# Gating's second half moved to the end of the step, with its weights one step later, and the maxima transferred from another queue

## The reference

```
xn  = layernorm(x)
a   = softmax(rot(q) rot(k)^T / sqrt(8) + decay, causal) v      # 16 heads of 8
n1  = layernorm(xn) * w + b
rw  = gating(n1)                    # (tokens, 8 experts)
q, k, v = sum_e rw[e] * (n1 @ proj[e])
hs  = xn + sum_e rw[e] * (softmax(q k^T, causal) v) @ o_proj[e]
out = x + a @ Wo + hs + moe(layernorm(hs))

gating: l = normalize(n1) @ normalize(sim) - sigmoid(g)
        keep l > 0, or, where none is, the two largest l
        softmax over what is kept
```

## Time and profile before

| | |
|---|---|
| three runs | 1439.68 us median, 1435.52 to 1447.45 |
| profiled execution | 1432.54 us, its span 1430.7 us |
| PE busy | 1284.3 us, 90% of the span |
| PEld busy | 1016.5 us, 71% |
| DVE busy | 1021.5 us, 71% |
| ACT busy | 762.4 us, 53% |
| GpSimd busy | 221.6 us, 15% |

### The profile page before, as it was taken

One profiled execution on the slowest core, in us unless ns is written; L12 is line 12 of the kernel. 1 busy time (PEld: TensorE's weight loads), 2 busy tenths in 40 slices (PEclk: granted clock), 3 DMA queues, 4 the chain that ended last, 5 costly groups with the idle time before them and its releaser, 6 DMA issues.

```text
span 1430.7 us, 33751 instructions
## 1 busy us (share of the span) xinstructions
PE 1284.3 (90%) x10686; PEld 1016.5 (71%) x10780; DVE 1021.5 (71%) x3882; ACT 762.4 (53%) x1664; POOL 221.6 (15%) x326
## 2 busy tenths in 40 slices
PE   0369999999999999999999999999999979999999
PEld 0247777777778777777777777777777767777776
DVE  8557777777777777777777777777776656677754
ACT  1125655665555555555555555555555574455532
POOL 4011112111122211111111111112111200000000
PEclk9679999999999999999999999999999999999999
DMA  4423233223333333333222233223223204554344
GB/s 117 94 54 85 76 77 76 75 76 80 79 85 79 78 76 79 83 90 90 77 75 76 75 83 80 76 75 76 75 76 77 58 9 172 204 202 153 149 153 159
DMA packets 89904, 133.33 MB, mean 93 GB/s; under 512 B 9675, under 2 KB 78395, under 8 KB 78523
## 3 DMA queue, kind: packets, MB, share of 16 engines
q1 hardware_dynamic: 89298, 132.10, 32.6%
q10 hardware_dynamic: 488, 0.01, 0.0%
HBM read 108.76 MB, written 21.50 MB: 91 GB/s over the span
## 4 chain that ended last, share of the span: by engine, by line
PE 63%; DVE 15%; DMA 11%; issue 6%; ACT 4%; DVEq 1%; SPq 0%; ACTq 0%
DMA qst<-mT 10%; PE ps L1663 8%; PE ps L1649 8%; PE ps L1401 7%; PE ps L1402 6%; PE ps L1411 6%; PE ps L1275 4%; PE ps L1379 4%; DVE mx L1025 3%; PE ps L1337 3%; PE ps L1360 3%; PE ps L1333 2%; PE ps L1330 2%; PE ps L1436 1%; PE ps L1383 1%
## 5 line engine op out<-in xcount | busy, mean ns | idle before, releaser
L629 ACT ACTIVATE pr<-ps 128x512 f32<-128x512 f32 x384 | 227.7, 593 | 205.4 <-PE ps L1360 166.7
L1025 DVE TENSOR_REDUCE mx<-ps 128x2 f32<-128x512 f32 (+1 forms) x384 | 263.9, 688 | 46.6 <-PE ps L1330 26.2
L634 ACT ACTIVATE ps<-trn 128x512 f32<-128x512 bf16 x382 | 229.8, 601 | 12.1
L530 POOL TENSOR_TENSOR n1s<-rep,n1T 128x256 f32<-128x256 f32 x256 | 177.0, 730 | 277.4 <-DVE mpart L1037 252.9
L1663 PEld LDWEIGHTS ps<-w2s,ats 128*128 128x128 f32 x1024 | 131.7, 192 | 50.4 <-issue 46.5
L1401 PE MATMUL ps<-n1s,wq 128*128 128x256 f32 x512 | 160.6, 396 | 0.0
L1402 PE MATMUL ps<-n1s,wk 128*128 128x256 f32 x512 | 152.8, 380 | 0.0
L1411 PE MATMUL ps<-wv,n1s 128*128 128x128 f32 x1024 | 150.6, 280 | 0.0
L803 ACT ACTIVATE n1s<-ps 128x512 f32<-128x512 f32 x128 | 76.5, 597 | 123.3 <-PE ps L1649 122.1
L1411 PEld LDWEIGHTS ps<-wv,n1s 128*128 128x128 f32 x1024 | 131.9, 192 | 9.0 <-issue 6.3
L1663 PE MATMUL ps<-w2s,ats 128*128 128x128 f32 x1024 | 135.7, 276 | 1.1 <-DVE ats L1207 1.1
(11 more groups left out here) (225 smaller groups left out, 2281.6 us busy)
## 6 DMA issues: line engine op xcount, KB each, us to landing
rep<-scr_rw SPq DMA_DIRECT2D x32, 1024.0 KB, 5.0
qst<-scr_rw SPq DMA_DIRECT2D x16, 1024.0 KB, 6.5
kst<-scr_rw SPq DMA_DIRECT2D x16, 1024.0 KB, 8.3
scr_parts<-parts SPq DMA_DIRECT2D x64, 192.0 KB, 2.3
qst<-scr_parts SPq DMA_DIRECT2D x192, 64.0 KB
kst<-scr_parts SPq DMA_DIRECT2D x32, 192.0 KB
xt<-in_x SPq DMA_DIRECT2D x32, 128.0 KB, 2.3
kst<-scr_parts SPq DMA_DIRECT2D x32, 128.0 KB
```

What stands on the lines that cost most here:

```text
L530: pool.tensor_tensor(n1s[:, e], rep[:, par, e], n1T[:, par], ALU.mult).then_inc(n1s_done, 1)
L629: act.activation(pr[:, G % 2, i], ps[:, S2[k % 2]], ACT.Exp).then_inc(exp_done, 1)
L634: act.activation(ps[:, S2[k % 2]], seeds[:, 1 if (k + 2) % 3 == 2 else 0], ACT.Copy).then_inc(seed_done, 1)
L1025: dve.tensor_reduce(mx[:, min(i, 1), h:h + n], ps[:, S1[k % 2]].rearrange("p (h t) -> p h t", h=n), AX_X, ALU.max, negate=True).then_inc(s ...
```

## The change

Gating is cut in two. `gating_head` runs to the tanh's input in its old place, and only maxima 4 to 6 are put beside it. `gating_tail` runs at the end of the step, behind `add_x`, with `add_hs` put in behind link 24. `soft_max` now follows the layer norm, ahead of maxima 7 to 10, and `soft_norm` follows `max_parts`. The weights go through PE, ACT and SP one step later: `weights_T`, `evac_weights` and `store_weights` of sequence n + 1 stand early in step n, using the bank `PVB`, and `pv` of the step waits for the copy (`rwT_done`). `max_T` moves ahead of `soft_av`, `evac_max` ahead of `evac_v`, and the transfer of `mT` is issued by ACT itself instead of SP.

```diff
-GATE_MAX_AT = (3, 7, 10, 14, 18, 21, 24)
+GATE_MAX_AT = (3, 7, 10)
+HS_AT = 24
@@ SP, step
                 if n_x:
+                    store_weights(n + 1, 1 - u)
                     spread_weights(n + 1, 1 - u)
...
                     stacks(n + 2, u, True)
-                    store_weights(n + 2, u)
-                if n_x:
-                    put_max(n + 1, 1 - u)
@@ ACT
-            def evac_max(b):
+            def evac_max(b, par):
...
                 act.activation(mT[:], ps[0:3 * H, S1[0], 0:S // 2].bitcast(BF16), ACT.Copy).then_inc(mT_done, 1)
+                act.wait_ge(mT_done, b + 1)
+                act.dma_start(qst[R_MAX:R_MAX + 3, par], mT[:]).then_inc(max_in, 16)
@@ ACT, step
                     exps(n, k, n_x == 0)
+                    if n_x and k == 1:
+                        evac_weights(n + 1)
...
                 evac_ve(n)
+                if n_x:
+                    evac_max(n + 1, 1 - u)
                 if n_x >= 2:
-                    evac_weights(n + 2)
                     evac_v(n + 2, u)
-                if n_x:
-                    evac_max(n + 1)
@@ DVE, step
+                def beside_tail(k):
+                    if k == HS_AT:
+                        add_hs(n, u)
...
                     next_max(3)
-                    gating(n + 2, T, 0, gate1, LG1, NORM1, 1, beside_gating)
+                    c = gating_head(n + 2, T, 0, gate1, LG1, NORM1, beside_head)
                     run(norm)
...
+                if n_x:
+                    soft_max(n)
+                    next_max(7)
+                    next_max(8)
+                    next_max(9)
+                    next_max(10)
...
                 next_max(11)
                 if n_x:
                     max_parts(n + 1)
+                    soft_norm(n)
...
                 add_x(n, u)
-                add_hs(n, u)
+                if n_x >= 2:
+                    c.beside = beside_tail
+                    gating_tail(c, n + 2, T, gate1, 1)
+                else:
+                    add_hs(n, u)
@@ PE
+                if not isinstance(b, int) or b:
+
+                    pe.wait_ge(xa_done, b - 1)
+                pe.transpose(ps[0:E * T, PVB, 0:P], gt[:, 6, 0:T].rearrange("p i e -> p (i e)"), ident[:]
@@ PE, pv
                     pe.wait_ge(xa_done, n)
+                    pe.wait_ge(rwT_done, min(n + 2, NB) if isinstance(n, int) else n + 2)
@@ PE, step
                 qk(n, 1)
+                if n_x:
+                    weights_T(n + 1)
...
                 out_T(n, 1)
+                if n_x:
+                    max_T(n + 1)
                 soft_av(n, (lambda: pe.wait_ge(lg_read, f + 1)) if n_x >= 2 else (lambda: None))
                 if n_x >= 2:
-                    weights_T(f, True)
                     proj_v(f, True)
-                if n_x:
-                    max_T(n + 1)
```

More of the change, by code:

```diff
@@ L447, in _ @@
             stacks(1, 1, False)
-            store_weights(1, 1)
-            put_max(0, 0)
             step(0, 0, 3)
@@ L976, in gating, with gating_tail @@
                 dve.tensor_tensor(Dm, L, bc(m1), ALU.subtract).then_inc(tanh_in, 1)
+                return c
+            def gating_tail(c, b, nt, q, groups):
+                chain, lg_out, lg_read, tanh_in, tanh_out, rwT_out, rw_out = q
+                bc, (L, Dm, A, B2, C2_, F), (m1, m2, mc, rn, ina, tot) = gate_views(nt)
+                th = gt[:, 9, 0:nt]
+                rk = rank[:].rearrange("p (o e) -> p o e", o=1).broadcast_to((P, nt, E))
                 dve.wait_ge(tanh_in, b + 1)
@@ L1009, in gating @@
                 c.close()
+            def gating(b, nt, which, q, lg, norm, groups, beside=None):
+                gating_tail(gating_head(b, nt, which, q, lg, norm, beside), b, nt, q, groups)
             LG1 = ps[:, G0, 0:T * LG_W].rearrange("p (i k) -> p i k", k=LG_W)
@@ L1313, in unit1 @@
                 G, i = divmod(k, 3)
-                if k == 1:
-                    pe.wait_ge(rwT_done, b + 1 if not isinstance(b, int) or b else 2)
                 if k == 0:
```

58 lines of the change are left out of this document (26 added, 32 removed).

## The result

The changed kernel takes 1452.24 us (median of 17 runs, 1446.99 to 1456.51); the kernel before, on the same chips, 1438.37 (17 runs, 1435.43 to 1447.45). The ratio is 1.0092, with a 95% interval of 1.0079 to 1.0105: slower by about 0.9%, where 1412 us was predicted, in a range of 1401 to 1434. The profiled executions say the same: a span of 1449.9 us against 1430.7, 19.2 more. A profile is one execution, up to 6 us away from its kernel's median (before: 1432.54 against 1438.37), so lengths of steps read from it are good to about 0.2 us.

A forecast was written before the change was run, and what follows sets the result against it. PE, busy 90%, was taken as the bound, with waits for the maxima's transfer and DVE's maxima. Per step 0.9 + 0.4 + 0.15 − 0.2 − 0.3 = 0.95, 28 us over 29 steps, from 1439.7: 1412 us, range 1401 to 1434.

The forecast's parts named there:

- 0.9 for the transfer: PE's wait at each step's first `unit2` for `qst<-mT` goes by issuing it 2.3 us earlier: 0.9 us per step gained.
- first rival: The maxima's transfer is still late, held by the stacks' backlog: 6 us gained, 1434 us; chance 0.12.
- With the loop's landing times of 4.6 to 5.6 it arrives at 671.2 to 672.2: Maxima's transfer, issued at about 666.55, lands before PE needs it at 672.4, so the wait of 0.9 goes.
- 0.4 for the maxima: PE's 0.45 us wait per step at `unit1` for DVE's maxima nearly goes: 0.4 gained, bounds 0.2 to 0.45.
- 0.2 per step that was feared at unit 9: Maximum 7 comes later, behind the softmax maxima, so PE may lose 0.2 us at unit 9.
- −0.3 for the wait at `weights_T`: PE waits there for the gating tail's `rw_out`, slowed by GpSimd's overlap: 0.3 us per step lost, bounds 0 to 0.7.
- the prediction's signs: What the profile after should show, here L981 to L984 taking 0.3 to 0.5 each in turn while GpSimd runs.
- 0.15 − 0.2 for the moved transposes: On PE, 0.15 us per step gained between `soft_av` and `oe`, 0.2 lost by `weights_T` behind `qk(n, 1)`.
- The tail's length: Gating's second half on DVE at the step's end runs from 670.05 to `rw_out` at about 675.9.
- It had 2 us of slack to the second `proj`, so nothing on PE moves: DVE's rotation in the next step starts at 675.9 instead of 674.85, at no cost to PE.
- The last part after the steps is untouched: The work after the steps was taken to stay as it was, with no term in the sum.
- The forecast's step of 33.2: Length of a looped step expected in the profile after, in us, against 34.12 before.

The follow-up runs named there:

- e3: Changed kernel with the transfer of `mT` issued by SP again, behind the stacks; 1451.83 us, 1.0101 of the kernel before.
- e7: e1 without the six q-stack transfers of every step, so part of the computation is left out; 1404.24 us, 0.9776 of the kernel before.
- e1: Changed kernel with DVE's loop written out, other engines keeping theirs; 1429.84 us, 0.9944 of the kernel before.
- v7: v4 with maximum 7 ahead of `soft_max` instead of behind it; 1388.46 us, 0.9676 of the kernel before.
- e2: Kernel before with DVE's loop written out; 1428.59 us, 0.9931 of the kernel before.
- v1: Changed kernel with DVE's loop written out and stacks sent in two 48-row transfers, parts stored already repeated; 1406.35 us, 0.9795 of the kernel before.
- v4: v1 with `weights_T` moved behind `logits_T` and ACT's copy behind exp 2; 1389.92 us, 0.9686 of the kernel before.
- v2: Kernel before with DVE's loop written out and stacks sent in two 48-row transfers, parts stored already repeated; 1385.15 us, 0.9644 of the kernel before.
- v6: v2 with DVE's loop put back; 1395.27 us, 0.9727 of the kernel before.
- v5: v1 with DVE's loop put back; 1436.94 us, 1.0011 of the kernel before.
- e4: Changed kernel with SP's stacks held until the maxima's copy `mT` is done; 1550.66 us, 1.0782 of the kernel before.
- e9: Changed kernel with four steps instead of two in DVE's loop body, steps 26 and 27 written out; 1452.21 us, 1.0111 of the kernel before.
- e6: e1 with the maxima's transfer cut into three of 16 rows; 1435.03 us, 0.9991 of the kernel before.

## Why the prediction was wrong

By its own terms, per step:

- **0.9 for the transfer: failed.** This is the first rival's mechanism, given 0.12, though its 1434 us is 18 short of the time. The step that failed is "With the loop's landing times of 4.6 to 5.6 it arrives at 671.2 to 672.2". These times were taken as a property of the transfer, while they were that of the point at which it met the stacks. Issued 2.2 us earlier, it took 2 us longer, on either queue (e3), and without the q stack it did not matter at all (e7). The prediction had the number that says so in its own rows, 2.92 alone against 4.6 to 5.6 in the loop, and weighed the new queue against it. The Trainium skill's rule (DMA: Bandwidth & Descriptors, "Issuing engines are not separate DMA queues") would have decided this rightly: e3 agrees with it.
- **0.4 for the maxima: at its lower bound, and in full only without the loop.** PE's 5.9 us in 26 waits at L1345 are the 0.2 per step that was feared at unit 9, so 0.2 of the 0.4 came. In e1 the wait is gone (PEld 1.7 us in all), and v7 showed that there is then next to nothing to lose at unit 9. The forecast had a shorter wait by moving links; what is left of it comes with the loop. More than half of the wait was the loop's in the kernel before, too: PEld 17.1 us there and 7.2 in e2.
- **−0.3 for the wait at `weights_T`, bounds 0 and 0.7: right where it can be seen.** In the changed kernel it is hidden behind the late transfer (as the first rival said), and in e7 and v1, without that, it is 0.58, in the upper part of the bounds. The cause is GpSimd, and 0.8 us is what it adds to the tail; 0.6 to 0.8 were forecast. It does not fall on four instructions in turn, as the prediction's signs have it, but on the two with two inputs.
- **0.15 − 0.2 for the moved transposes: not measured by themselves.** With the waits of the two kernels mended their steps are equal (32.6 in v4 and v7, 32.65 in v2), so together they are near the forecast's nothing.
- **The tail's length: right.** "ten more instructions, `rw_out` at about 675.9": L981 to L1009 take 645.52 to 651.3, so 5.8, and the forecast was 670.05 to 675.9.
- **"It had 2 us of slack to the second `proj`, so nothing on PE moves": failed, and it made the sign.** The 2.12 us of idle time was read in a step without a turn. In the twelve with a turn it is 2.5 to 3.2 in the kernel before, and by v6's 2.6 us the turn fills nearly all of it. All but one of these rows name PE as what ended it, which hides the turn; the one that does not was in the trace:

```profile
437.02 0.69 DVE L942 TENSOR_TENSOR rott<-ps,cs 128x512 f32<-128x512 f32 x1 [2.55 <-issue]
```

In the changed kernel DVE has its tail to do first and spends 3.1 to 3.6 us at the turn after it, which the slack does not hold. With the tail ended at 651.3, the rotation starts at 654.9 instead of right behind it. The list of DVE's instructions has the loop there, and one step of each parity had to be looked at.
- **"The last part after the steps is untouched": failed.** Step 30 does not gate, but the change rebuilt its list on DVE, and it takes 5.0 us more. The sum has nothing for it, and gives no reason.

The sum, in the medians: without DVE's loop the change costs 1.2 us (e1 1429.84, e2 1428.59), the 5 us or less of step 30 included. The loop adds 22.4 in the changed kernel and 9.8 in the kernel before, so 12.6 more. Together this is the 13.9 that was to be explained, by its making; the test is whether the turns fit the 12.6. They are 12 x 1.2 = 14.4 by the steps of the trace. With the wide stacks the loop adds 30.6 (v5 over v1) and 10.1 (v6 over v2), so 20.5 more, and the turns are 12 x 1.7 = 20.4. What is left of the loop's cost, 8 to 10 us in all four kernels, is the 0.3 to 0.4 in every step; where it arises is shown, its cause stays open.

The forecast's step of 33.2 is what the changed kernel does once backlog and loop are away (33.22 in e7 and in v1). But the kernel before does 32.65 then. Both waits that the change aimed at go away at less cost by other means, the transfer's by wider stacks, the maxima's largely by writing out DVE's loop. With two of its faults mended (v4 and v7, 1390 and 1388) the change equals v2's 1385 in the looped steps and loses in step 30; with that mended too it would be about level with v2 (an estimate: 1388 less 5 is 1383), but this was not run.

## What to carry to other kernels

A transfer that takes 5 us in the loop and 3 alone may be ended by what moves beside it. Here it was: issuing it earlier or from another engine bought nothing, and making the others fewer and wider took the wait away. An engine's loop is work too, at one place of its list: before something is moved ahead of that place, look there, in a step with the turn, how much idle time covers it. And before a stall is attacked by rearranging three engines, take away its suspected cause in one experiment; here wide stacks alone (v6) were worth 2.7%, and 3.6% with DVE's loop written out (v2). Where a change also rewrites the steps at the end of the pipeline, read these by themselves: a window over the loop does not have them.

## What the hardware showed that I had not expected

- A turn of DVE's loop takes 2.6 to 3.6 us from the last instruction to the next, with a body of two steps, 3.9 to 5.9 where transfers run beside it (e4), and 4.2 to 4.6 with a body of four (e9; 12 and 5 turns in the traces). Fewer, longer turns cost as much in all.
- Besides, a loop on DVE makes each of its steps longer by 0.3 to 0.4 us, turn or not (34.1 against 33.8; 33.0 against 32.65), although the same arithmetic runs.
- The stacks' 768 KB in two transfers of 48 rows, with the parts repeated in DRAM, no longer delay the transfer behind them as nine did, although the DMA queue of SP is busier over the span (35.7% of the engines' time in v1 against 32.7% in e1).
- After 4 us without work, in e4, TensorE's granted clock went from full to half for some 7 us. The waits of up to 2 us in the changed kernel and the one before left it at full (1.00 from 120 to 1080).
- Three issues in a row on ACT hold it for 2.7 us (e6), where one takes 0.73.
